# Writing fp8 activations straight from VectorE's clamp instead of converting them on ScalarE

## The reference

```python
xn = layernorm(x)
# Mamba: 1024 channels, 16 states each
dA  = exp(A[None, :, None, :] * dt[:, :, :, None])
dBu = (dt[:, :, :, None] * Bm[:, None, :, :]) * hs[:, :, :, None]
h_t = dA_t * h_(t-1) + dBu_t          # scan over 512 positions
y_t = sum over the states of h_t * C_t
# feed-forward, products of fp8 numbers, results in bf16
ff_gate = dot(fp8(xn), fp8(w_gating[0]))
ff1     = dot(fp8(xn), fp8(w_gating[1]))
activations = gelu(ff_gate) * ff1     # bf16, 2048 hidden features
outputs = dot(fp8(activations), fp8(w_linear))
x = x + mamba(xn) + outputs
```

## Time and profile before

| | |
|---|---|
| three runs | 1084.03, 1084.43, 1085.84 us; median 1084.43 us |
| the profiled execution | 1084.43 us |
| its span | 1082.6 us |
| PE, DVE, ACT, POOL busy | 86%, 94%, 77%, 83% of the span |
| granted TensorE clock, mean | 0.939 of full speed |

### The profile page before, as it was taken

The page is one execution under the profiler, slowest core; times in us unless marked ns, Lnnn a source line. Parts: engine busy times, 40 slices in busy tenths (PEclk is TensorE's granted clock), DMA queues, the critical chain, the costliest instruction groups (busy, mean ns, idle before and its releaser), DMA issues.

```text
span 1082.6 us, 14656 instructions
## 1 busy us (share of the span) xinstructions
PE 926.4 (86%) x4318; PEld 574.6 (53%) x4328; DVE 1018.7 (94%) x1214; ACT 829.2 (77%) x1154; POOL 893.2 (83%) x496
## 2 busy tenths in 40 slices
PE   3978899868778997898889979987998799879998
PEld 2746566435555555455545545555555455545554
DVE  6979898599999999999999999999999999999996
ACT  3777877678889865888897668988966689889662
POOL 4344535699999899989998999899989989998993
PEclk9999999888888998999989988999899899989999
DMA  7687778992111218432212193421212923212101
GB/s 280 186 272 236 291 220 320 353 371 107 53 59 40 87 47 272 179 125 73 78 37 88 40 320 118 136 78 59 71 57 71 345 87 102 78 59 78 40 0 39
DMA packets 53157, 150.24 MB, mean 139 GB/s; under 512 B 5728, under 2 KB 14048, under 8 KB 50016
## 3 DMA queue, kind: packets, MB, share of 16 engines
q1 hardware_dynamic: 53088, 149.41, 39.5%
HBM read 111.37 MB, written 38.01 MB: 138 GB/s over the span
## 4 chain that ended last, share of the span: by engine, by line
DVE 36%; issue 29%; ACT 18%; PE 10%; POOL 5%; DVEq 1%; DMA 1%; POOLq 0%
DVE da L1100 14%; DVE prod L1075 10%; DVE hp L1100 8%; ACT da L994 5%; ACT gate_bf L972 3%; PE yT L1226 3%; POOL dt_du L371 3%; ACT L973 2%; ACT L972 2%; DVE y L1083 2%; ACT L983 2%; ACT L982 2%; POOL hs_lo L366 2%; PE mm L1175 1%; DVE gate_bf L1113 1%
## 5 line engine op out<-in xcount | busy, mean ns | idle before, releaser
L994 ACT ACTIVATE da<-unit,neg_a 128x512 f32<-128x512 f32 x512 | 339.8, 684 | 162.6 <-DVE prod L1075 159.6
L833 POOL TENSOR_TENSOR dbu<-unit,b_head 128x1024 f32<-128x1024 f32 x192 | 449.8, 2370 | 0.0
L1100 DVE TENSOR_TENSOR_SCAN da<-da,dbu 128x512 f32<-128x512 f32 x352 | 416.9, 1214 | 1.2
L1226 PE MATMUL yT<-ident,prod 128*128 128x128 f32 x1408 | 232.8, 296 | 97.7 <-DVE prod L1075 97.1
L1226 PEld LDWEIGHTS yT<-ident,prod 128*128 128x128 f32 x1408 | 176.7, 151 | 225.6 <-DVE prod L1075 175.1
L1063 POOL TENSOR_TENSOR hp<-hp,c_head 128x512 f32<-128x512 f32 x128 | 163.6, 1278 | 58.0 <-DVE gate_bf L1116 53.4
L1100 DVE TENSOR_TENSOR_SCAN hp<-da,dbu 128x512 f32<-128x512 f32 x160 | 193.0, 1206 | 9.5 <-ACT da L994 9.5
L1075 DVE TENSOR_TENSOR prod<-da,c_head 128x512 f32<-128x512 f32 x256 | 170.4, 666 | 0.0
L1175 PE MATMUL mm<-xn_b,w_sb 128*128 128x512 fp8e4 x512 | 150.0, 428 | 3.8 <-ACT gate_bf L1009 2.7
L833 POOL TENSOR_TENSOR dbu<-unit,b_all 128x1024 f32<-128x1024 f32 x64 | 151.4, 2366 | 0.0
L1187 PE MATMUL mm<-xnT_b,wgate 128*128 128x512 f32 x256 | 128.9, 601 | 2.0 <-ACT gate_bf L1009 1.7
(11 more groups left out here) (118 smaller groups left out, 1281.7 us busy)
## 6 DMA issues: line engine op xcount, KB each, us to landing
unit<-unit_d SPq DMA_DIRECT2D x32, 768.0 KB, 4.3
unit_d<-dt_du SPq DMA_DIRECT2D x32, 512.0 KB, 2.7
wf<-in_wffn SPq DMA_DIRECT2D x12, 1024.0 KB, 6.6
c_head<-bc_d SPq DMA_DIRECT2D x24, 512.0 KB, 4.1
b_head<-bc_d SPq DMA_DIRECT2D x18, 512.0 KB, 4.9
unit_d<-hs SPq DMA_DIRECT2D x32, 256.0 KB, 6.4
w_sb<-w_d SPq DMA_DIRECT2D x64, 128.0 KB, 3.9
wgate<-in_win_gate SPq DMA_DIRECT2D x32, 256.0 KB, 2.7
```

The lines of the kernel that those rows point to most:

```text
L833: return nc.gpsimd.tensor_tensor(dbu[:, n % DBUS:n % DBUS + NS, :], twice, b_all[n // NS], ALU.mult)
L994: nc.scalar.activation(da[n % SLOTS][:, :], unit[:, k % 2, 0, :], ACT.Exp, scale=neg_a[:, k, n:n + 1]).then_inc(da_ready, 1)
L1100: nc.vector.tensor_tensor_scan(state, da[n % SLOTS][:, :], dbu[:, n % DBUS, :], 0.0, ALU.mult, ALU.add).then_inc(scanned, 1)
L1226: ins = nc.tensor.matmul(yT[k % 2][:, t * P:(t + 1) * P], product[:, t * P:(t + 1) * P], ident[:, :], start=False, stop=last, is_transpose ...
```

## The change

DVE's clamp no longer writes bf16 back in place: it writes fp8 into `act8` itself. ACT's conversion is dropped, and with it the semaphore `clamped`. POOL, which waited for `clamped`, now waits for `act8_ready`, which the clamp raises. Whoever waited for `act8_ready` before still does.

```diff
-GELU_USED, PORT_GIVEN, FP8_MADE = 4, 4, 8
+GELU_USED, PORT_GIVEN = 4, 4
...
-                    if n == FP8_MADE and 1 <= k <= FFN_UNITS:
-                        act.wait_ge(clamped, b * FFN_UNITS + k)
-                        act.sem_inc(waited, 1)
-                        nc.scalar.activation(act8[:, sum(HIDS[:k - 1]):sum(HIDS[:k]), :].bitcast(FP8), gate_bf[:, 0:HIDS[k - 1], :],
-                                             ACT.Copy, saturate=False).then_inc(act8_ready, 1)
...
                         if 1 <= k <= FFN_UNITS and m == PORT_GIVEN:
-                            pool.wait_ge(clamped, b * FFN_UNITS + k)
+                            pool.wait_ge(act8_ready, b * FFN_UNITS + k)
...
-                        nc.vector.tensor_scalar(tiles, tiles, FP8_MAX, -FP8_MAX, ALU.min, ALU.max).then_inc(clamped, 1)
+                        nc.vector.tensor_scalar(act8[:, sum(HIDS[:k - 1]):sum(HIDS[:k]), :].bitcast(FP8), gate_bf[:, 0:HIDS[k - 1], :],
+                                                FP8_MAX, -FP8_MAX, ALU.min, ALU.max, saturate=False).then_inc(act8_ready, 1)
```

More of the change, by code:

```diff
@@ L778, in stage_b @@
         ffn_mm, ffn_copied, gelu_ready = sem("ffn_mm"), sem("ffn_copied"), sem("gelu_ready")
-        act_bf_ready, clamped, act8_ready = sem("act_bf_ready"), sem("clamped"), sem("act8_ready")
+        act_bf_ready, act8_ready = sem("act_bf_ready"), sem("act8_ready")
         lin_mm, lin_copied = sem("lin_mm"), sem("lin_copied")
```

## The result

The changed kernel takes 1092.58 us (median of 4 runs, 1091.71 to 1093.44), the kernel before 1084.24 us in the same comparison (4 runs, 1084.03 to 1085.84). The ratio is 1.0075, with a 95% interval of 1.0061 to 1.0087: 8.3 us slower, where 8.5 us were forecast and 1092.9 us predicted.

A forecast was written before the change was run, and what follows sets the result against it. The prediction took DVE to bound the kernel: 1084.4 us, plus 8.5 for the slower fp8 clamps, zero for removing ACT's conversion and nothing for GpSimd's moved wait, gives 1092.9 us, range 1091 to 1097.

The forecast's parts named there:

- DVE sets the pace: From 235 us on, DVE is the bound: only 12.7 us of recurring gaps in some 840 us, so added time hardly hides.
- The removal counts zero: Dropping ACT's conversion, 31.1 us of ACT's time, gains nothing; DVE takes the next `da` without a wait, ACT 1.6 us early.
- The clamp's price: DVE's 20 clamps go from 560 to 956 ns (x16) and 695 to 1226 ns (x4): 8.5 us more.
- The rival with the old pace: DVE's fp8 clamps stay at 560 and 695 ns because the input is bf16: 1084.4 us; chance 5%.
- The rival of one element at a time: DVE's fp8 clamps process one element at a time, 29.6 us more: 1114.0 us; chance 4%.
- the case of three tiles charged like four: DVE's 1536-element clamps cost as much as 2048-element ones: 12.8 us more, 1097 us, the range's upper end.
- POOL's slack: POOL's restart and DVE's next scan both come 0.4 us later; the 1.3 us before DVE needs `dbu` stays, adding nothing.
- Contention: Rival: GpSimd (POOL) working in SBUF disturbs DVE's clamps, 20 x 0.87 = 17.3 us more, 1110.2 us; chance 2%.
- The sum: All 20 clamps stand in DVE's unbroken order and delay the end: 1084.4 + 8.5 = 1092.9 us.

## Why the prediction was right

*DVE sets the pace.* Right, and now shown from both sides: 8.5 us more of clamp made the kernel 8.3 us slower, and 15 us less made it 13.4 faster.

*The removal counts zero.* Right. The bf16 version without ACT's conversion stands within 0.1% of the kernel before; the kernel with both the conversion and the fp8 clamp is as slow as the changed one. ACT's waits for DVE rose from 153.5 to 194.3 us, 40.8 against the 31.1 + 8.5 = 39.6 that were forecast.

*The clamp's price.* 956 and 1226 ns were worked out from a float cast and the float to fp8 clamp; 960 and 1228 were measured. By the two sizes that is (1228 - 960) / 512 = 0.52 ns per element and some 156 ns fixed, against 0.26 and 155 with a bf16 output. That a cast of 512 elements lay on the same line was an assumption, and it held. The rival with the old pace, for which the bf16 input spoke, is out. The trace agrees with the rule of the Trainium skill, "VectorE: DVE Perf Modes", section "What auto-detection actually checks", of 16-bit types on both sides for the fastest pace: both sizes fit it, and the 560 ns came back with the bf16 output. One thing stays open: the edit changed the output's type and its tile at once (`act8` instead of in place), and no run writes bf16 into another tile, so the runs alone don't separate the two. The rival of one element at a time is out too, and so is the case of three tiles charged like four.

*POOL's slack.* Right: no wait of DVE for `dbu` in the changed kernel from 235 us on, and 62.4 us of waiting for the clamp where about 62 were forecast.

*Contention.* The rival had 17.3 us as its price if POOL ran under the clamps. The two runs without the wait show that this was far too low: 54.1 and 58.1 us. The case didn't arise, because POOL's wait hangs on the end of the same instruction; its low chance was right for the reason given. Its price was mis-sized: it took 0.87 us, one long row of stage A, for the price of a meeting. That row follows the same pattern as the others: the weight clamp at 33.19 found a POOL product with 1.01 us left (32.91 + 1.29 = 34.20). The activations' clamp found a `dbu` with 2.05 us left, and the multiply, which the price left out, met POOL too.

*The sum.* 8.5 forecast, 8.3 measured by the medians, 8.8 by the two traces from the first scan on.

## What to carry to other kernels

Moving the end of a computation from an engine that waits to the engine that is waited for cost its full price there, however much the relieved engine saved; read who waits for whom before the busy shares. Folding a type conversion into an instruction that runs anyway is free only if the instruction keeps its pace: this one, fp8 into `act8` instead of bf16 in place, took twice the time per element. Where two engines take turns, look at what the other one is doing at the moment of the start: the price is the rest of its instruction. And the idle time of a second engine is no room by itself: subtract what the unit will be shorter, and the time for which it has to be idle.

## What was not expected of the hardware

A multiply or clamp of DVE that starts while a POOL instruction runs is lengthened by the rest of that instruction less some 0.14 us, however short it is itself: 1904 ns on a clamp of 560 ns and 1906 ns on one of 960, with 2.05 us of a `dbu` left; 716 ns on the multiply in front of them, with 0.85 us of a product left; 0 to 0.9 us on the multiply where it was moved. This holds in all 120 places of the four runs in which the two could meet, and in the two long weight clamps of stage A in the trace of before (2.09 and 1.56 us instead of 1.22, with 1.01 and 0.47 us of a POOL instruction left). POOL's `dbu` in turn wait for DVE. POOL's own clamp, with one bf16 input, took 1466 ns for 1536 elements and 1892 for 2048, 0.83 ns per element, against 1278 ns for a product of 512 elements with two float inputs. ACT's saturating copy ran at the pace of the plain one, 1484 ns for 1536 elements, but each use brought two table loads of 1283 ns.
